# A four-stage transformer kernel: weighting moved ahead of a placing in the delta-rule stage, and the last layer's first transpositions moved ahead of a projection

## The chip, the cores and the metric

The kernel runs on one core of one Trainium2 chip. The time is the device time of one execution in microseconds (us). It was run three times for the median, and one further execution was profiled. The profile names the engines of the core: PE (TensorE, matrix products), DVE (VectorE), ACT (ScalarE), POOL (GpSimd), and SP, which only issues transfers. Each engine runs its own instructions strictly in the order of its queue, and the engines meet through semaphores, so a wait at the head of a queue holds everything behind it.

## The reference, cut to what matters

Four layers run one after the other over 2048 tokens of 128 features (two batches of 1024 tokens): an attention, a gated feed-forward network, a delta-rule layer with convolutions, and a network of sign weights. Each is followed by a residual addition and a layer norm. The change touches the third layer and the first steps of the fourth.

```python
# third layer; per batch and head: L = 1024 tokens in 32 chunks of 32 tokens
def body(S, inp):                       # a scan over the 32 chunks
    q_i, k_i, u_i, w_i = inp
    attn = jnp.where(tri, jnp.einsum('bhcd,bhed->bhce', q_i, k_i), 0.0)
    u_i = u_i - w_i @ S
    o_i = q_i @ S + attn @ u_i
    S = S + jnp.einsum('bhcd,bhce->bhde', k_i, u_i)
    return (S, o_i)
...
local_short = causal_dwconv(vf, fir_short)      # filter of 3 taps over the values
local_long = causal_dwconv(vf, fir_long)        # filter of 31 taps
p = jax.nn.softmax(logits, axis=-1)
local_mix = p[..., 0:1] * v + p[..., 1:2] * local_short + p[..., 2:3] * local_long
o = w_global[..., None] * delta_out + (1.0 - w_global)[..., None] * local_mix
o = o * jax.lax.rsqrt(jnp.mean(o * o, -1, keepdims=True) + EPS) * rms_w
x = _layernorm(x + o.reshape(Bx, Lx, H * DV) @ Wo)
# fourth layer
h = jnp.concatenate([x, -x], axis=-1)
h = s0 * _conn_dense(k0, h)             # weights +1 or -1 from k0; then relu, two more products
```

## The kernel before, in words

All instructions are written out by hand, one list for each engine, with explicit semaphores; no scheduler changes their order. The two batches of the delta rule go through the same steps, first batch 0, then batch 1. For one batch, in the order of the data:

1. PE multiplies by the inverse matrices (`times_inverse`, L1893), ACT copies the result, called u and w, to SBUF (`copy_uw`, L746).
2. DVE and ACT place the u parts into a block layout, one half each (`place_u`, L524), and PE forms the inputs of the state (`inputs_of_state`, L1903), which ACT copies out (`copy_b`, L753).
3. PE forms the products of the transitions (L1914). DVE makes the matrix of each step and corrects the queries from them (`transitions`, L1331 and L1336).
4. PE starts the outputs of batch 0 (`begin_outputs`, L1927, four groups of 16 products ahead of the scan).

Then one scan of 31 steps serves both batches: in each step PE multiplies the state (L1994), DVE adds the step's input (L1445; step 0 is the copy L1442), and PE puts products of outputs behind each state product (L1961 and L1927). The scan can begin when DVE has made its first copy, L1442.

Beside this path lies the local mix. The filters' results stand in `filtered` in token layout. DVE multiplies their weights in (`weigh(i)`, L1345, two instructions of 128x512 for each of four groups of 512 tokens; the groups come in the order `FINAL = (0, 2, 1, 3)`, so `weigh(0)` and `weigh(1)` serve the token groups 0 and 2). POOL multiplies the values by their weights (L1019, four instructions), and adds the two filters to them (L1029 and L1030, two instructions for each group). What comes of this is first used late in the scan, by `blend_local`. DVE also forms the first sign weights of the last layer, `sw0` (L1356).

Toward the end of the scan and behind it, for each group i of tokens: ACT and DVE norm the outputs, PE transposes them (`o_to_features`, L1974), ACT copies them (`load_oT`, L798), PE projects (`project`, L1983, two instructions for each of four tiles), DVE adds the residual and takes the statistics (`add_y4` L1390, `stats3` L1396 and L1399), POOL forms the reciprocal root, and DVE norms (`norm3`, L1407). The last layer then begins with PE's transpositions (`x3_transposes`, L2034), which ACT and DVE split into a leading part and a rest (`transposed`, L802 on ACT, L1418 on DVE). PE's first products are `first` (L2044, L2045) and `hidden` (L2056, L2057), with ACT's relu (L807) and DVE's rest (`rests`, L1423) between them. For group 0 the transposed rows use the bank in which `o_to_features` writes, so PE waits there for `oT_ready` 2 as well as for `x3_ready` 1.

## Time and profile before

| | |
|---|---|
| median of three runs | 609.99 us |
| lowest and highest | 609.53 and 613.34 us |
| the profiled execution's own time | 612.65 us |
| its span, first to last instruction | 610.9 us |
| busy in the span: PE, DVE, ACT, POOL | 545.2, 406.9, 324.7, 175.1 us |
| the chain that ended last, by engine | PE 71%, DVE 10%, DMA 7%, ACT 7%, issue 3% |
| mean granted clock of PE | 0.932 of full |

The profiled execution lies 2.66 us above the median, and 1.75 us of its time lie outside its span. Busy times are means over stages with different limits, so they don't tell what a change in one stage is worth. In the rows below, a row of the timeline gives the start, the duration, the engine, the line of the kernel, what is written and read, the number of instructions that are merged in it, and in square brackets the idle time ahead of it with what ended it.

### The profile page before, as it was taken

What the parts mean: (1) busy time and instruction counts of PE and PEld (TensorE: products, weight loads), DVE (VectorE), ACT (ScalarE), POOL (GpSimd) and SP (SyncE); (2) the same over time, 40 slices, a digit from 0 to 9 for tenths busy, and PEclk for the clock granted to TensorE, in tenths of its full rate; (3) what the DMA queues carried; (4) which work ended last, traced back from release to release, by engine and by line L of the source; (5) the groups of instructions that cost most, each with busy time, mean ns of one, the idle gap of its engine ahead of it and who ended that gap; (6) DMA issues with size and microseconds to landing.
All of it is one profiled execution on the core that took longest, in us unless ns stands there. A gap on an engine that the chain in (4) does not pass through costs nothing.

```text
span 610.9 us, 17361 instructions
## 1 busy us (share of the span) xinstructions
PE 545.2 (89%) x7412; PEld 377.7 (62%) x7412; DVE 406.9 (67%) x773; ACT 324.7 (53%) x574; POOL 175.1 (29%) x333
## 2 busy tenths in 40 slices
PE   4699999999999999999999996996998659888993
PEld 2345555555555557877777774774676658666672
DVE  5697989999999825263634437447798572576774
ACT  2327888887888875656555544656605300134441
POOL 7000111445445421010101024238980370010101
PEclk9999999999999999999999998997999665559998
DMA  4778657374250000010000000032734100000011
GB/s 116 149 216 208 191 142 162 68 162 67 62 100 4 5 2 1 0 28 10 0 2 1 1 0 1 2 70 38 139 75 85 23 3 4 5 1 0 2 34 34
DMA packets 54050, 33.80 MB, mean 55 GB/s; under 512 B 38853, under 2 KB 45509, under 8 KB 53974
## 3 DMA queue, kind: packets, MB, share of 16 engines
q1 hardware_dynamic: 48822, 31.65, 23.0%
q10 hardware_dynamic: 5152, 1.05, 1.1%
q8 instruction: 58, 0.95, 0.7%
q14 instruction: 18, 0.15, 0.1%
HBM read 20.83 MB, written 9.44 MB: 50 GB/s over the span
## 4 chain that ended last, share of the span: by engine, by line
PE 71%; DVE 10%; DMA 7%; ACT 7%; issue 3%; SPq 1%; POOL 1%; POOLq 0%; ACTq 0%; DVEq 0%
PE ps L1761 9%; PE ps L1746 8%; PE ps L1513 7%; PE ps L1515 6%; PE ps L1514 6%; PE ps L1861 6%; DMA qst<-shift_sb 5%; PE ps L1725 3%; PE ps L1927 2%; PE ps L2056 2%; PE ps L2057 2%; PE ps L1893 2%; ACT prob L682 2%; PE ps L1994 2%; PE ps L1603 1%
## 5 line engine op out<-in xcount | busy, mean ns | idle before, releaser
L1204 DVE TENSOR_REDUCE nmx<-ps 128x1 f32<-128x1024 f32 x128 | 154.1, 1217 | 19.4 <-PE ps L1726 17.9
L682 ACT ACTIVATE prob<-ps 128x512 f32<-128x512 f32 x256 | 137.5, 597 | 27.0 <-PE ps L1746 26.8
L1761 PE MATMUL ps<-prob,vp 128*32 128x128 f32 x2048 | 78.9, 278 | 0.0
L1746 PE MATMUL ps<-qst,kst 50*128 50x512 f32 x256 | 73.6, 492 | 4.9 <-ACT prob L682 3.4
L1761 PEld LDWEIGHTS ps<-prob,vp 128*32 128x32 f32 x2048 | 49.1, 109 | 39.8 <-ACT prob L682 22.6
L1077 DVE TENSOR_TENSOR h_lo<-hf,h_hi 128x512 fp32r<-128x512 f32 x48 | 33.1, 689 | 52.5 <-ACT h_hi L591 50.2
L1513 PE MATMUL ps<-h_hi,w_lo 128*128 128x512 f32 x144 | 58.2, 404 | 2.4 <-DVE h_lo L1077 2.4
L1515 PE MATMUL ps<-h_hi,w_hi 128*128 128x512 f32 x144 | 56.9, 395 | 0.0
L1514 PE MATMUL ps<-h_lo,w_hi 128*128 128x512 f32 x144 | 56.8, 394 | 0.0
L1725 PE MATMUL ps<-kst,qst 48*128 48x512 f32 x128 | 53.0, 415 | 3.4 <-DMA kst<-k_scratch 3.3
L1726 PE MATMUL ps<-kst,qst 48*128 48x512 f32 x128 | 51.7, 405 | 0.0
L1746 PEld LDWEIGHTS ps<-qst,kst 50*128 50x128 f32 x256 | 29.3, 183 | 35.0 <-ACT prob L682 22.9
L590 ACT ACTIVATE hf<-ps,ffn_scale 128x512 f32<-128x512 f32 x32 | 22.1, 690 | 34.3 <-PE ps L1515 32.7
L852 POOL TENSOR_SCALAR rs<-mv 128x4 f32<-128x4 f32 x8 | 3.0, 376 | 122.4 <-DVE mv L1055 122.3
L1861 PE MATMUL ps<-vpad,fir_diag 32*32 32x512 f32 x1088 | 37.0, 618 | 0.4 <-DVE ka L1139 0.4
L891 POOL CAST nsplit<-nmx 128x4 fp32r<-128x4 f32 x32 | 6.0, 188 | 106.7 <-DVE nmx L1204 104.4
L1513 PEld LDWEIGHTS ps<-h_hi,w_lo 128*128 128x128 f32 x144 | 27.0, 188 | 11.6 <-issue 4.0
L1423 DVE SCALAR_TENSOR_TENSOR h_lo<-ps,h_hi 128x512 fp32r<-128x512 f32 x32 | 21.2, 684 | 16.4 <-ACT h_hi L807 16.4
L1861 PEld LDWEIGHTS ps<-vpad,fir_diag 32*32 32x32 f32 x1088 | 23.9, 105 | 12.3 <-issue 3.8
L1515 PEld LDWEIGHTS ps<-h_hi,w_hi 128*128 128x128 f32 x144 | 27.0, 188 | 6.7
L1514 PEld LDWEIGHTS ps<-h_lo,w_hi 128*128 128x128 f32 x144 | 27.1, 188 | 6.0
L807 ACT ACTIVATE h_hi<-ps 128x512 fp32r<-128x512 f32 x32 | 18.0, 598 | 23.2 <-PE ps L2057 18.0
(248 smaller groups left out, 1107.5 us busy)
## 6 DMA issues: line engine op xcount, KB each, us to landing
qst<-q_scratch SPq DMA_DIRECT2D x31, 192.0 KB, 4.4
kst<-k_scratch SPq DMA_DIRECT2D x31, 192.0 KB, 5.0
w_raw<-L_ffn_h_w SPq DMA_DIRECT2D x8, 256.0 KB, 3.4
kd<-ka SPq DMA_DIRECT2D x8, 256.0 KB, 6.2
X<-L_attn_x SPq DMA_DIRECT2D x4, 256.0 KB, 5.3
qst<-shift_sb SPq DMA_DIRECT2D x64, 4.0 KB
q_scratch<-w_hi SPq DMA_DIRECT2D x2, 512.0 KB, 5.5
k_scratch<-w_lo SPq DMA_DIRECT2D x2, 512.0 KB, 3.1
```

The source lines that it names most:

```text
L590: nc.scalar.activation(hf[:, o, :], bank, ACT.Gelu, scale=scale)
L682: nc.scalar.activation(prob[:, n % PROBS, GT * (t % 2):GT * (t % 2) + GT], ps[:, RINGB + i % RING, :], ACT.Exp, scale=SCORE_SCALE).then_in ...
L1077: nc.vector.tensor_tensor(h2_lo[:, layer, o, :], hf[:, o, :], h2_hi[:, layer, o, :].bitcast(F32), ALU.subtract).then_inc(lo2_ready, 1)
L1204: nc.vector.tensor_reduce(nmx[:, u % 2, j:j + 1], pair, AX.X, ALU.max, negate=True).then_inc(max_done, 1)
L1513: nc.tensor.matmul(out, wl, xh, start=start, stop=False)
L1514: nc.tensor.matmul(out, wh, xl, start=False, stop=False)
L1515: return nc.tensor.matmul(out, wh, xh, start=False, stop=stop)
L1725: nc.tensor.matmul(ps[:, bank, :], qst[0:48, p, P * k:P * k + P], kst[0:48, p, 0:GT], start=True, stop=True)
L1726: nc.tensor.matmul(ps[:, bank + 1, :], qst[64:112, p, P * k:P * k + P], kst[64:112, p, GT:S], start=True, stop=True).then_inc(max_psum, 1)
L1746: nc.tensor.matmul(ps[:, RINGB + i % RING, :], kst[r:r + 50, p, P * t:P * t + P], half_of(qst[r:r + 50, p, :], u % 2), start=True, stop=Tr ...
L1761: last = nc.tensor.matmul(ps[32 * j:32 * j + 32, PVB, P * half:P * half + P], vp[:, h, t, :], prob[:, n % PROBS, c:c + P], start=(t == 0), ...
L1861: last = nc.tensor.matmul(ps[32 * g:32 * g + 32, FIR_BANK[k] + h, :], fir_diag[f, (0, FIRL)[k] + t, :], vpad[f, g // 2, off:off + GT], sta ...
```

## The change

Nothing is computed differently; instructions change places in three of the queues.

```diff
@@ POOL: the memset of the state and the wait for the corrected queries
-            pool.wait_ge(uw_psum, B)
-            nc.gpsimd.memset(state[:, 0], 0.0).then_inc(state_zeroed, 1)
-            pool.wait_ge(g_ready, 2)
             for i, g in enumerate(FINAL):
+                if i == 2:
+                    pool.wait_ge(uw_psum, B)
+                    nc.gpsimd.memset(state[:, 0], 0.0).then_inc(state_zeroed, 1)
+                    pool.wait_ge(g_ready, 2)
@@ DVE: before the scan
             weigh(0)
             weigh(1)
+            weigh(2)
+            weigh(3)
+            dve.wait_ge(signs_in, 16 * 6)
+            nc.vector.tensor_tensor(sw0[:], k0[:, 0, :], k0[:, 1, :], ALU.subtract)
             place_u(nc.vector.tensor_copy, dve, 1, (2, 3))
             transitions(1)
-            dve.wait_ge(signs_in, 16 * 6)
-            nc.vector.tensor_tensor(sw0[:], k0[:, 0, :], k0[:, 1, :], ALU.subtract)
-            weigh(2)
-            weigh(3)
@@ DVE: behind the scan
             norm3(0)
+            transposed(0)
             add_y4(1)
             stats3(1)
-            transposed(0)
             rests(0, 0, range(FB))
@@ PE: in the scan
-                if j == 29:
+                if j == 28:
                     project(0, (0, 1))
-                if j == 30:
+                if j == 29:
                     project(0, (2, 3))
@@ PE: behind the scan
+            x3_transposes(0)
             project(1, (0, 1, 2, 3))
-            x3_transposes(0)
             first(0)
```

On DVE, ahead of the scan, the queue of the kernel before reads as follows. `low<-inv_flat` is `place_u` of batch 1, `sw` is the last layer's sign weights, and `state<-prep` is the scan's first step.

```order
L1345 TENSOR_TENSOR filtered<-filtered,mixw 128x4x4x32 x3
L524 COPY low<-inv_flat 32x32x32 [waits b_psum0,low_zeroed0,uw_ready0]
L524 COPY low<-inv_flat 32x32x32
L1331 TENSOR_TENSOR tT<-eye,ps 128x256 [waits mg_psum0]
L1331 TENSOR_TENSOR tT<-eye,ps 128x256 x3
L1336 TENSOR_TENSOR kq<-kq,ps 128x8x32 x4
L1356 TENSOR_TENSOR sw<-k 128x512 [waits x_in1]
L1345 TENSOR_TENSOR filtered<-filtered,mixw 128x4x4x32 x4
L1442 COPY state<-prep 128x64 [waits b_ready0]
```

The same place in the changed kernel (line numbers are one higher there):

```order
L1346 TENSOR_TENSOR filtered<-filtered,mixw 128x4x4x32 x7
L1357 TENSOR_TENSOR sw<-k 128x512 [waits x_in1]
L524 COPY low<-inv_flat 32x32x32 [waits b_psum0,low_zeroed0,uw_ready0]
L524 COPY low<-inv_flat 32x32x32
L1332 TENSOR_TENSOR tT<-eye,ps 128x256 [waits mg_psum0]
L1332 TENSOR_TENSOR tT<-eye,ps 128x256 x3
L1337 TENSOR_TENSOR kq<-kq,ps 128x8x32 x4
L1443 COPY state<-prep 128x64 [waits b_ready0]
```

Four weighting instructions and the one on the signs have moved from between the transitions and the first state to ahead of the placing.

On POOL, in the same stretch, the kernel before has the memset ahead of all additions of the filters:

```order
L1019 TENSOR_TENSOR vtok<-vtok,mixw 128x512 x3
L1024 MEMSET state 128x64 [waits uw_psum0,pool_step]
L1029 TENSOR_TENSOR vtok<-vtok,filtered 128x512 [waits weighted0,g_ready0]
L1030 TENSOR_TENSOR vtok<-vtok,filtered 128x512 [waits pool_step]
L1029 TENSOR_TENSOR vtok<-vtok,filtered 128x512 [waits weighted0]
```

The changed kernel there:

```order
L1019 TENSOR_TENSOR vtok<-vtok,mixw 128x512 x3
L1030 TENSOR_TENSOR vtok<-vtok,filtered 128x512 [waits weighted0,pool_step]
L1031 TENSOR_TENSOR vtok<-vtok,filtered 128x512 [waits pool_step]
L1030 TENSOR_TENSOR vtok<-vtok,filtered 128x512 [waits weighted0]
L1031 TENSOR_TENSOR vtok<-vtok,filtered 128x512 [waits pool_step]
L1026 MEMSET state 128x64 [waits uw_psum0]
L1030 TENSOR_TENSOR vtok<-vtok,filtered 128x512 [waits weighted0,g_ready0]
```

Four of the eight additions now stand ahead of the memset and need only `weighted`.

On PE, behind the scan, the kernel before projects group 1 (`ps<-wo,vk`) and then transposes the normed rows (`ps<-ident,X`):

```order
L1974 MATMUL ps<-ident,low 128x128 x3
L1983 MATMUL ps<-wo,vk 128x128 [waits y4_added0,oT_ready0]
L1983 MATMUL ps<-wo,vk 128x128 x3
L2034 MATMUL ps<-ident,X 128x128 [waits oT_ready0,x3_ready0]
L2034 MATMUL ps<-ident,X 128x128 x3
L2044 MATMUL ps<-x_lo,sw 128x512 [waits x3T_lo0,x3T_hi0]
```

The changed kernel there:

```order
L1975 MATMUL ps<-ident,low 128x128 x3
L2035 MATMUL ps<-ident,X 128x128 [waits oT_ready0,x3_ready0]
L2035 MATMUL ps<-ident,X 128x128 x3
L1984 MATMUL ps<-wo,vk 128x128 [waits y4_added0,oT_ready0]
L1984 MATMUL ps<-wo,vk 128x128 x3
L2045 MATMUL ps<-x_lo,sw 128x512 [waits x3T_lo0,x3T_hi0]
```

The wait for the normed rows now stands ahead of the projection of group 1.

## Rows read from the trace of the kernel before

**Rows 1.** Timeline of DVE ahead of the scan, 424 to 530 us.

```profile
473.93 5.10 DVE L1345 TENSOR_TENSOR filtered<-filtered,mixw 128x512 f32<-128x512 f32 x4
486.21 1.39 DVE L524 COPY low<-inv_flat 32x1024 f32<-32x1024 f32 x2 [7.19 <-ACT inv_flat L746]
...
488.96 1.40 DVE L1336 TENSOR_TENSOR kq<-kq,ps 128x256 f32<-128x256 f32 x4
490.29 0.68 DVE L1356 TENSOR_TENSOR sw<-k 128x512 fp32r<-128x512 uint8 x1
490.89 6.76 DVE L1345 TENSOR_TENSOR filtered<-filtered,mixw 128x512 f32<-128x512 f32 x4
497.57 1.25 DVE L1442 COPY state<-prep 128x64 f32<-128x64 f32 x1
```

**Rows 2.** Timeline of PE in the same stretch.

```profile
490.51 0.54 PE L1927 MATMUL ps<-inv_flat,kd 64*64 64x32 f32 x12 [0.66 <-DVE kq L1336]
491.81 1.70 PE L1927 MATMUL ps<-inv_flat,kd 64*64 64x32 f32 x52 [0.76 <-issue]
498.96 0.44 PE L1994 MATMUL ps<-state,tT 32*32 32x32 f32 x16 [5.45 <-DVE state L1442]
```

**Rows 3.** Timeline of ACT, ahead of the scan and at its end.

```profile
489.89 1.20 ACT L753 COPY prep<-ps 128x256 f32<-128x256 f32 x4 [1.58 <-PE ps L1903]
...
530.18 0.59 ACT L798 COPY vk<-ps 128x512 f32<-128x512 f32 x1 [1.74 <-PE ps L1974]
```

**Rows 4.** Timeline of POOL ahead of the scan and at its start.

```profile
474.15 5.80 POOL L1019 TENSOR_TENSOR vtok<-vtok,mixw 128x512 f32<-128x512 f32 x4 [16.66 <-DVE kq L1336]
...
490.44 1.65 POOL L1029 TENSOR_TENSOR vtok<-vtok,filtered 128x512 f32<-128x512 f32 x1 [6.08 <-DVE kq L1336]
...
501.42 1.27 POOL L1030 TENSOR_TENSOR vtok<-vtok,filtered 128x512 f32<-128x512 f32 x1
```

**Rows 5.** Windows: busy us of five engines, then granted PE clock, DMA share, GB/s.

```profile
484.00:493.00 9.00, 5.35 (x311) 4.74 (x311) 6.75 (x13) 5.34 (x10) 2.63 (x3) 1.00 0.02 5
493.00:494.00 1.00, 0.51 (x17) 0.40 (x13) 1.00 (x1) 0.00 (x0) 1.00 (x2) 0.72 0.00 0
499.00:542.00 43.00, 37.13 (x1212) 30.98 (x1212) 18.30 (x67) 4.17 (x9) 5.37 (x7) 0.50 0.02 4
542.00:548.00 6.00, 5.86 (x14) 4.63 (x15) 3.52 (x8) 2.39 (x4) 0.81 (x1) 0.50 0.01 3
548.00:560.00 12.00, 9.77 (x50) 7.50 (x48) 7.41 (x14) 6.77 (x15) 0.00 (x0) 1.00 0.00 0
```

**Rows 6.** The chain that ended last, in a step of the scan: start, us, what.

```profile
505.54 0.57 PE ps L1927 x8
```

**Rows 7.** Timeline of PE at the end of the scan and behind it.

```profile
531.29 1.22 PE L1983 MATMUL ps<-wo,vk 128*128 128x128 f32 x4
...
532.87 1.22 PE L1983 MATMUL ps<-wo,vk 128*128 128x128 f32 x4
...
537.23 2.08 PE L1983 MATMUL ps<-wo,vk 128*128 128x128 f32 x8 [0.67 <-ACT vk L798]
539.10 1.06 PE L2034 MATMUL ps<-ident,X 128*128 128x128 f32 x4
542.14 0.76 PE L2044 MATMUL ps<-x_lo,sw 128*128 128x512 f32 x1 [1.98 <-DVE x_lo L1418]
```

**Rows 8.** Timeline of DVE in the same stretch.

```profile
532.95 0.23 DVE L1445 TENSOR_TENSOR state<-ps,prep 128x64 f32<-128x64 f32 x1 [1.35 <-PE ps L1994]
...
537.63 1.12 DVE L1407 TENSOR_SCALAR X<-X,mv,rs 128x128 f32<-128x128 f32 x4 [0.20 <-POOL rs L1036]
539.35 0.69 DVE L1390 TENSOR_TENSOR X<-X,ps 128x512 f32<-128x512 f32 x1 [0.60 <-PE ps L1983]
...
541.27 0.72 DVE L1418 SCALAR_TENSOR_TENSOR x_lo<-ps,s_sign,x_lo 128x512 fp32r<-128x512 f32 x1
544.00 0.69 DVE L1423 SCALAR_TENSOR_TENSOR h_lo<-ps,h_hi 128x512 fp32r<-128x512 f32 x1 [2.00 <-ACT h_hi L807]
```

More of the change, by code:

```diff
@@ L2016, in _ @@
                     o_to_features(0, (2, 3))
+                if j == 28:
+                    project(0, (0, 1))
                 if j == 29:
-                    project(0, (0, 1))
-                if j == 30:
                     project(0, (2, 3))
```

## The prediction, made before the changed kernel ran

> **What bounds the kernel now.** I first read the chain of waits, to find who holds the stage that the change touches. Ahead of the scan it passes from PE to DVE: through `transitions(1)`, the sign weights, the second weighting, and the first copy of the state, and only then back to PE. The timelines of the engines show the same. DVE ends L1336 at 490.36, then works for 0.68 us on the signs, 6.76 us on the weighting and 1.25 us on the copy [rows 1]. PE has ended its last product ahead of the scan at 493.51, and waits 5.45 us for that copy [rows 2]. The inputs of the state have been with DVE since 491.09 [rows 3]. So the 7.4 us on signs and weighting are on the path only as far as they reach past PE's own work, 5.45 us. The reader should also see the hole on DVE before that: from 479.03 to 486.21 it waits 7.19 us for ACT's copies [rows 1]. That is where the change puts this work.
>
> The second thing to see is that DVE and POOL hold each other up. A 128x512 instruction with two operands in SBUF took 0.68 us when it began ahead of POOL's addition (the signs, L1356); the weighting, of the same size, took 6.76/4 = 1.69 us each beside POOL's additions and 5.10/4 = 1.28 us beside POOL's L1019 [rows 1, 4]. POOL's addition takes 1.65 us beside DVE's weighting and 1.27 us when DVE leaves it alone [rows 4].
>
> The third view is the clock of PE. It is granted at 1.00 (2.4 GHz) from 484 to 493, falls within the microsecond from 493 to 494 (mean 0.72), and stays at 0.50 (1.2 GHz) through the whole scan and behind it until 548, from where it is 1.00 again [rows 5]. A mean of 0.72 puts the fall at 493 + (0.72 - 0.5)/0.5 = 493.4, ahead of the 5.45 us of idleness. So it is not this idleness that brings it down.
>
> **Part 1, the weighting and the signs ahead of the placing.** On DVE they begin at 479.03. POOL's last L1019 is then still running, until 479.95 [rows 4]. Then POOL starts its four additions of groups 0 and 1, whose weights are in; in the kernel before they waited for `g_ready` 2 until 490.44. This is the part of the move that the gap doesn't show: five instructions of DVE that would need 5 x 0.68 = 3.4 us alone stand beside five of POOL's. At the measured pace of a pair, 1.65 to 1.69 us, POOL's four end at 479.95 + 4 x 1.67 = 486.6. The signs, as DVE's fifth, are held by the fourth addition and end most of their own 0.68 us behind it, an estimate of 487.1. The placing began at 486.21, so it is 0.9 us later. Its bounds: nothing, if DVE isn't held up beyond 486.2 (five at the 1.28 us of the L1019 rows end at 485.4), and 1.3 us if all five take 1.69 us (487.5). I take 0.9, because L1029 and L1030 are the very instructions that POOL runs there.
>
> Beside the measured pace stands a rule of the Trainium skill. Its page "SBUF — State Buffer", section "SBUF: two separate sides", says that the port pair which DVE and POOL share is locked for a whole instruction, and that the loser fully blocks. By that rule a pair takes the sum of both engines' own times, 0.68 + 1.27 = 1.95 us, which is rival A below. The trace agrees with the direction and not quite with the size: 1.65 to 1.69 us for a pair.
>
> The placing on DVE moves to 487.1 to 488.5. ACT's half of it ended at 488.31 anyway, so PE's L1903 is 0.2 us later and the inputs of the state are ready near 491.3. The transitions follow the placing: from its start to the end of L1336 it was 490.36 - 486.21 = 4.15 us, now 487.1 + 4.15 = 491.25. PE's 64 products of L1927 therefore begin at 491.4 instead of 490.51, and need 3.0 us with the 0.76 us gap that they have [rows 2]: to 494.4. The state's copy is only 64 columns wide. It took 1.25 us since POOL was in the midst of an addition; in the worst case it takes the same now, from 491.3 to 492.6, and hides behind L1927. POOL's memset comes behind its four additions, near 486.8, and PE asks for it only behind L1927. The scan starts at about 494.45 instead of 498.96: **-4.5 us**.
>
> One thing takes part of it back. If the clock falls at 493.4 as before, what is left of L1927 (1.0 us) runs at half rate: 8 of them take 0.57 us, 71 ns each [rows 6], against 1.70/52 = 33 ns each. That is +1.1 us. It cost nothing in the kernel before, because 5.45 us of waiting covered it. When the fall comes nearly a whole L1927 earlier, the price is 64 x 38 ns = 2.4 us; when it comes later, 0. I take half of 1.1 us, **+0.6**.
>
> The scan itself keeps its instructions and, by the rows, its clock of 0.50. POOL's last four additions, now 1.27 us each with nothing beside them, end early in the scan, long before `blend_local` needs them. The state additions of DVE took 0.23 us with or without POOL.
>
> **Part 2, project(0) one step earlier.** The step-28 place on PE is reached at 530.7. ACT's copy of what is projected ends at 530.77 [rows 3], so PE waits about 0.15 us there. Moreover the last addition of the state was hidden under the second projection: DVE did it from 532.95 to 533.18 while PE projected until 534.02 [rows 7, 8]. With both projections gone from there, PE waits 0.2 us for it. In return, the projection is out before the last addition, so `add_y4(0)` starts right behind it: 534.3 instead of 534.12. The sum is 0.2 us later for the residual path and 0.3 for PE: **+0.2**.
>
> **Part 3, transpositions ahead of project(1), and transposed(0) ahead of add_y4(1).** Before, PE projected group 1 from 537.23, while DVE normed group 0 (537.63 to 538.75), transposed until 540.16, and then waited 1.98 us for L1418, which stood behind `add_y4(1)` and its statistics on DVE, 539.35 to 541.35 [rows 7, 8]. Now PE waits from about 536.9 for the norm, to 538.95, transposes in 1.06 us, projects in 2.08 us, and is at 542.05. ACT and DVE have split the rows by 541.6 meanwhile. `first(0)` thus begins at 542.05 against 542.14. The 1.98 us wait is gone, and a wait of about the same length ahead of the transpositions has taken its place; PE has the same work between the norm and the first product. Behind that, `add_y4(1)` and the statistics (2.0 us) now run from 542.1 to 544.1; the first `rests` was ready at 544.00 [rows 8], so 0.1 us at most comes back. This part is **-0.1** (part 2's 0.2 us are already in those times, so both together are -0.1). Its bounds: +0.4, if `rests` is late for all of `hidden`, and -1.5, if the clock returns sooner because PE now works from 539 on without a pause.
>
> **The sum.** -4.5 + 0.6 - 0.1 = -4.0 us. Against the profiled execution's own 612.65 us this gives 608.6; it lies 2.66 us above the median, and nothing in the terms depends on that offset, so against the median it is 609.99 - 4.0 = **606.0 us**, 0.7% faster.
>
> **Rivals.**
>
> A. *The contention eats more* (0.15). Each of DVE's five instructions waits for a whole addition of POOL: five pairs of 0.68 + 1.27 = 1.95 us from 479.03 end at 488.8, and the placing is late by 2.6 us instead of 0.9. For it: POOL's additions now stand exactly in DVE's old hole. Against: the pairs of before took 1.69 us. The gain is 4.0 - 1.7 = 2.3 us, **607.7 us**.
>
> B. *The clock stays at 2.4 GHz into the scan* (0.10). The only long idleness of PE ahead of the scan goes. Products of L1927 would then take 33 ns instead of 71 in the first steps and the 16 with eight each, (48 + 128) x 38 ns = 6.7 us less at the most, of which I take 4 to be on the path, since part of it would only turn into waiting for DVE's addition. That gives **602 us**. Against: the clock fell before that idleness, and 43 us of scan in which PE was busy for 37.13 us did not bring it back [rows 5]. The Trainium skill, "TensorE: Matmul & The Clock Gate", section "What's actually happening", holds that activity releases the throttle and that the gate follows how busy PE has been. By that rule removing the idleness should keep the clock; the trace of the scan doesn't agree with its simple form, as small products that fill PE's row leave the clock at 0.50.
>
> C. *Nothing is gained* (0.08): the changed order does what it says, but the scan's early steps turn out to wait for something else, as for the inputs of the state, or the time comes back in the dense products behind the scan, which DVE's and ACT's chain bounds. **610 us**.
>
> D. *Slower* (0.05). The clock's return moves back. From 542 to 548 PE did 14 wide products in 5.86 us, 0.42 each, which at the full rate would be 0.21; and the clock returned only after these unbroken products from 542.14 on [rows 5, 7]. If the new wait ahead of the transpositions, with `rests` behind `add_y4(1)`, breaks that row up, each product at the lower rate costs 0.21 us. More than 19 of them cancel the 4 us; 33 would give -4 + 7 = +3, **613 us**. Against: the new order makes PE's row from the transpositions on longer, not shorter.
>
> **How the numbers follow.** The forecast has 0.62; within it the unknown terms (0 to 1.3 for the port, 0 to 2.4 for the clock, -1.5 to +0.4 for part 3) spread it from 603.5 to 608. For 8 in 10 I add rival A and most of B above 602: **602.0 to 609.0**. A measurement of this kernel can tell about 1% (6 us) from no change. Faster by more than that, below 603.9, is B and an eighth of the forecast case, with some of the noise: 0.20. Slower by that is D: 0.04. The rest, 0.76, is within 1%.
>
> **What would show it right or wrong.** In the changed profile: no wait of PE for L1443 above 1 us; DVE without its 7.19 us hole, its weighting at about 1.7 us each, and POOL's additions from 480 to 486.6; the placing near 487; the scan's first L1995 at 494 to 496; the clock at 0.50 through the scan; a wait of about 2 us ahead of L2035, and none ahead of L2045. I would be wrong above all if the clock in the scan is not 0.50, or if the port makes the placing later than 488.

## The result

The changed kernel took 606.17 us in the median of seven runs (604.1 to 607.3), against 609.99 us before, also in seven runs. The ratio is 0.9915, with a 95% interval from 0.9892 to 0.9938. That is 0.85% or 5 us less by the ratio and 3.8 us by the medians: a real gain, and one within the 1% that the prediction named. Ratios here and below leave disturbed runs out, so they can differ a little from the quotient of two medians.

The profiled execution of the changed kernel took 606.14 us with a span of 604.4, so 6.5 us less than the profiled one of before. The first thing to do with such a pair is to cut it at a place ahead of the change. ACT's second copy of u and w begins at 481.82 here; it began at 484.12 before (DVE's placing, right behind it, at 486.21 [rows 1]). That 2.30 us arose in parts that the change doesn't touch, and it is nearly the offset of the profiled execution of before above its median. From here on all stages are counted from this copy. Its row before:

```profile
484.12 2.05 ACT L746 COPY inv_flat<-ps 128x512 f32<-128x512 f32 x4 [7.99 <-PE ps L1893]
```

DVE ahead of the scan, in the changed kernel (timeline; all line numbers are one higher than before):

```profile
471.87 11.61 DVE L1346 TENSOR_TENSOR filtered<-filtered,mixw 128x512 f32<-128x512 f32 x8
483.40 1.77 DVE L1357 TENSOR_TENSOR sw<-k 128x512 fp32r<-128x512 uint8 x1
485.18 1.39 DVE L524 COPY low<-inv_flat 32x1024 f32<-32x1024 f32 x2
```

The hole of 7.19 us of before [rows 1] is gone: eight weightings in one row, the signs, and at once the placing. The signs took 1.77 us where they had taken 0.68. ACT's copies were out at 481.82 + 2.05 = 483.87; the placing begins at 485.18, so it is 1.3 us late.

POOL and ACT in the same stretch (two timelines):

```profile
472.10 5.79 POOL L1019 TENSOR_TENSOR vtok<-vtok,mixw 128x512 f32<-128x512 f32 x4 [16.79 <-DVE kq L1337]
477.97 1.60 POOL L1030 TENSOR_TENSOR vtok<-vtok,filtered 128x512 f32<-128x512 f32 x1
...
483.00 1.61 POOL L1031 TENSOR_TENSOR vtok<-vtok,filtered 128x512 f32<-128x512 f32 x1
...
489.42 1.27 POOL L1030 TENSOR_TENSOR vtok<-vtok,filtered 128x512 f32<-128x512 f32 x1 [4.72 <-DVE kq L1337]
```

```profile
481.82 2.05 ACT L746 COPY inv_flat<-ps 128x512 f32<-128x512 f32 x4 [8.39 <-PE ps L1894]
```

The first four additions lie from 477.97 to 484.61, at 1.6 to 1.7 us; the later ones, with nothing of DVE beside them, take 1.27 us, as in [rows 4].

PE ahead of the scan and the windows of its clock (busy us of five engines, granted clock, DMA share, GB/s):

```profile
486.62 1.69 PE L1904 MATMUL ps<-low,ka 64*32 64x64 f32 x128 [2.02 <-DVE low L524]
489.49 3.63 PE L1928 MATMUL ps<-inv_flat,kd 64*64 64x32 f32 x64 [1.18 <-DVE kq L1337]
493.04 0.44 PE L1995 MATMUL ps<-state,tT 32*32 32x32 f32 x16
```

```profile
484.00:493.00 9.00, 5.80 (x234) 5.30 (x224) 6.44 (x12) 3.20 (x6) 4.21 (x5) 0.70 0.01 4
...
499.00:536.00 37.00, 31.62 (x1065) 25.85 (x1064) 15.64 (x55) 4.17 (x9) 1.29 (x2) 0.50 0.02 4
```

PE no longer waits ahead of L1995; the 5.45 us of [rows 2] are gone. Its 64 products now run wholly at the lower clock, since the clock had fallen by then (a mean of 0.70 over the nine us from 484 puts the fall at 487.6): 3.55 us from their first to the scan, against 3.0 us with a gap inside before. From ACT's copy to the scan it is 11.22 us, against 14.84 before: 3.62 us less. The scan runs at 0.50 as before [rows 5].

The end of the scan and behind it, PE and then DVE:

```profile
533.03 1.11 PE L2035 MATMUL ps<-ident,X 128*128 128x128 f32 x4 [1.99 <-DVE X L1408]
533.94 1.92 PE L1984 MATMUL ps<-wo,vk 128*128 128x128 f32 x8
535.80 0.76 PE L2045 MATMUL ps<-x_lo,sw 128*128 128x512 f32 x1
```

```profile
523.71 0.22 DVE L1446 TENSOR_TENSOR state<-ps,prep 128x64 f32<-128x64 f32 x1 [1.40 <-PE ps L1995]
...
528.22 0.23 DVE L1446 TENSOR_TENSOR state<-ps,prep 128x64 f32<-128x64 f32 x1 [1.35 <-PE ps L1995]
528.37 0.68 DVE L1391 TENSOR_TENSOR X<-X,ps 128x512 f32<-128x512 f32 x1
...
531.86 1.12 DVE L1408 TENSOR_SCALAR X<-X,mv,rs 128x128 f32<-128x128 f32 x4 [0.20 <-POOL rs L1037]
534.91 0.75 DVE L1419 SCALAR_TENSOR_TENSOR x_lo<-ps,s_sign,x_lo 128x512 fp32r<-128x512 f32 x1 [1.93 <-ACT x_lo L802]
```

The residual's addition now follows the last state addition at once (528.37 behind 528.22); before it came 1.17 us behind it (534.12 against 532.95 [rows 8]). But the last steps are longer: the addition of step 27 (523.71) and the last one are 4.51 us apart, against 3.41 before (from 529.54 to 532.95). PE's wait of 1.99 us stands ahead of the transpositions, and the first wide product begins at 535.80 without a wait, 3.94 us behind the start of the norm. Before it was 542.14 - 537.63 = 4.51 us [rows 7, 8].

So the 6.5 us between the two profiles are: 2.30 ahead of the change, 3.62 up to the scan, 0.42 from the scan to the first wide product (43.18 us before, 42.76 now), and 0.16 from there to the end.

One thing behind the first wide product did change. The granted clock came back to 1.00 3.0 us behind that product, where it had taken 5.9 us before [rows 5]:

```profile
538.00:539.00 1.00, 1.00 (x4) 0.78 (x3) 0.96 (x2) 0.74 (x2) 0.92 (x2) 0.59 0.00 0
```

It fell once more, at 549.1, and was back at 552.5; before, it stayed at 1.00 there. From the first wide product to the end of the span it is 68.6 us now and 68.8 before.

### The profile page after: what moved, and what is told of

It is laid out like the page before. It is cut to its first block, busy times and chain, and to the rows that moved or that the text cites. A ratio compares the mean times of both kernels' runs of the same rounds, so it can differ in the third digit from the quotient of the medians.

```text
span 604.4 us, 17361 instructions
## 1 busy us (share of the span) xinstructions
PE 547.1 (91%) x7412; PEld 381.0 (63%) x7412; DVE 406.5 (67%) x773; ACT 325.0 (54%) x574; POOL 174.7 (29%) x333
## 4 chain that ended last, share of the span: by engine, by line
PE 72%; DVE 12%; ACT 6%; DMA 5%; issue 2%; POOL 1%; SPq 1%; POOLq 0%; ACTq 0%; DVEq 0%
PE ps L1762 10%; PE ps L1747 9%; PE ps L1514 7%; PE ps L1516 6%; PE ps L1515 6%; PE ps L1862 6%; DMA qst<-shift_sb 3%; PE ps L1928 3%; PE ps L1726 3%; PE ps L2057 2%; PE ps L2058 2%; DVE filtered L1346 2%; ACT prob L682 2%; PE ps L1995 1%; PE ps L1604 1%
```

## The experiments

Ten kernels. For each profile the same two stretches are read: from the start of ACT's second copy of u and w to the scan (**A**), and from there to the first wide product of the last layer (**B**). Two more columns give the clock of PE, from windows of 0.5 us: when it fell, counted from the same copy, and when it was back at 1.00, counted from the first wide product (below zero: ahead of it). The results of all are in one table, the readings behind it.

| kernel | ratio to before | 95% interval | A, us | placing behind ACT's copy started, us | B, us | clock fell, us | clock back, us |
|---|---|---|---|---|---|---|---|
| before | 1 | | 14.84 | 2.09 | 43.18 | 9.3 | 5.9 |
| changed | 0.9915 | 0.9892 to 0.9938 | 11.22 | 3.36 | 42.76 | 5.8 | 3.0 |
| e1, part 1 alone | 0.9931 | 0.9906 to 0.9957 | 9.43 | 2.09 | 42.78 | 9.1 | 4.7 |
| e2, parts 2 and 3 alone | 0.9979 | 0.9948 to 1.001 | 14.84 | 2.08 | 42.39 | 11.2 | 1.8 |
| e3, POOL as before | 0.9926 | 0.99 to 0.9952 | 10.73 | 2.09 | 42.10 | 9.4 | 0.9 |
| e4, filling ahead of the scan | 0.9912 | 0.988 to 0.9945 | 10.61 | 3.28 | 41.51 | 9.3 | 1.5 |
| e5, 512 columns a step | 1.0242 | 1.0216 to 1.0269 | 11.80 | 3.94 | 60.63 | 5.7 | 1.6 |
| e6, 256 columns a step | 1.0144 | 1.0116 to 1.0172 | 10.49 | 3.12 | 55.29 | 8.8 | 1.1 |
| e7, projection first | 0.9949 | 0.9929 to 0.9969 | 11.60 | 3.74 | 43.38 | 5.7 | -1.5 |
| e8, part 2 alone | one execution, 613.05 us | | 14.85 | 2.09 | 42.70 | 6.1 | 3.2 |
| e9, POOL's part alone | 0.9962 | 0.9937 to 0.9987 | 11.65 | 2.09 | 42.64 | 9.1 | 6.0 |
| e10, signs behind | 0.9919 | 0.9889 to 0.9948 | 9.63 | 2.09 | 42.08 | 8.9 | 1.5 |

Read A with care. The changed kernel, e1, e5, e6 and e7 have the same instructions up to the scan, and their A is 11.22, 9.43, 11.80, 10.49 and 11.60 us. A difference of up to some 2 us between two single profiles therefore shows nothing by itself. The three kernels with the old order up to the scan (before, e2, e8) all have 14.84 or 14.85 us.

**e1_part1: the work ahead of the scan alone.** The diffs on POOL and on DVE ahead of the scan, and nothing of the rest.

> Only the work ahead of the scan is moved: the second weighting and the signs ahead of the placing on DVE, four of POOL's additions ahead of its memset; all of the order behind the scan is that of the kernel before. Theory 1 (the gain comes from DVE's hole, and parts 2 and 3 are worth a few tenths): about 3.6 us faster than before, 606.4, the scan begins at about 494, and the first product of the last layer waits near 2 us for DVE's rest, as before. Theory 2 (a good part of the gain comes from the order behind the scan, because PE's clock returns sooner there): no more than 2.5 us faster, 607.5 or above.

0.9931, or 4.2 us less than before: the greater part of the change's gain. In the profile the first wide product waits 1.97 us for DVE's rest, as before. Theory 2, at most 2.5 us (a ratio of 0.9959), falls just outside the interval, which ends at 0.9957. A is 9.43 us, 1.8 less than in the changed kernel. DVE and PE of e1:

```profile
486.56 1.76 DVE L1357 TENSOR_TENSOR sw<-k 128x512 fp32r<-128x512 uint8 x1
488.58 1.39 DVE L524 COPY low<-inv_flat 32x1024 f32<-32x1024 f32 x2 [0.27 <-ACT inv_flat L746]
```

```profile
492.88 0.54 PE L1928 MATMUL ps<-inv_flat,kd 64*64 64x32 f32 x12 [0.66 <-DVE kq L1337]
494.17 1.82 PE L1928 MATMUL ps<-inv_flat,kd 64*64 64x32 f32 x52 [0.75 <-issue]
```

The weighting and signs took just as long (11.61 and 1.76 us). But here ACT's copy began 11.5 us behind the first weighting, against 9.95 us in the changed kernel, since PE had started its products with the inverse later. The hole was long enough, the placing waited for ACT and not for DVE, and PE's 64 products fell under the higher clock for the most part. The same code therefore loses between nothing and 1.9 us (e5's placing: 3.94 - 2.09) to the shared access, according to when the copies come.

**e2_parts23: the rest of the change alone.**

> The complement: the order ahead of the scan is that of the kernel before, the projections of group 0 stand one step earlier, and the transpositions of the last layer stand ahead of the projection of group 1. Theory 1: 0 to 0.4 us faster than before, 609.6 to 610. Theory 2: 1.3 us faster or more, 608.7 or below, with the granted clock back at 1.00 about 3 us sooner behind the first product than before.

0.9979, an interval that includes 1. The ratios alone can't settle it. The profile can: from the norm to the first wide product it takes 3.94 us (538.69 to 542.63), exactly as in the changed kernel and 0.57 less than before, and from the addition of step 27 to the norm 8.15 us against 8.09. So parts 2 and 3 are worth 0.5 us there, more than theory 1 had allowed and less than theory 2. The sign that theory 2 named did show: the clock was back 1.8 us behind the first wide product, 4.1 us sooner than before. But it fell again 12 us behind that product, which it did not do before, and from the first wide product to the end of the span e2 took 68.9 us, against 68.8.

**e3_pool_late: POOL in its old order.** In the changed kernel:

```diff
+            pool.wait_ge(uw_psum, B)
+            nc.gpsimd.memset(state[:, 0], 0.0).then_inc(state_zeroed, 1)
+            pool.wait_ge(g_ready, 2)
             for i, g in enumerate(FINAL):
-                if i == 2:
-                    pool.wait_ge(uw_psum, B)
-                    nc.gpsimd.memset(state[:, 0], 0.0).then_inc(state_zeroed, 1)
-                    pool.wait_ge(g_ready, 2)
```

> The changed kernel, but POOL keeps its old order: memset, the wait for the second correction of the queries, and then all eight additions. DVE's weighting then has only POOL's last multiplication beside it in the hole. Theory 1 (the shared access of DVE and POOL delays the placing by about 1.2 us in the changed kernel): the four weightings and the signs take 0.7 to 1.3 us each instead of 1.6 to 1.8, the placing begins as soon as ACT's copies are out, and the kernel is 0.5 to 1.2 us faster than the changed one, 605.0 to 605.7. Rival: the delay is hidden behind PE's products or paid back where POOL's eight additions meet the state's first copy: the same as the changed kernel, 606.2.

DVE of e3 (timeline):

```profile
473.94 8.38 DVE L1345 TENSOR_TENSOR filtered<-filtered,mixw 128x512 f32<-128x512 f32 x8
482.24 0.68 DVE L1356 TENSOR_TENSOR sw<-k 128x512 fp32r<-128x512 uint8 x1
487.90 1.39 DVE L524 COPY low<-inv_flat 32x1024 f32<-32x1024 f32 x2 [4.98 <-ACT inv_flat L746]
```

Without POOL's additions the eight weightings take 8.38 instead of 11.61 us and the signs 0.68 instead of 1.77; 4.98 us of the hole are left. This shows that the additions are what holds DVE up: 4.3 us over five instructions. The placing isn't late. Yet A is 10.73 us, where e1, whose placing wasn't late either, has 9.43. PE's 64 products have a gap of 1.58 us inside, for which the profile names no releaser (0.76 us in [rows 2], 0.75 in e1), and the last 52 of them took 2.29 us instead of 1.82, since more of them lay behind the fall of the clock. Those two make the 1.3 us. The ratio, 0.9926, does not tell e3 from the changed kernel; the 0.5 to 1.2 us that theory 1 expected are not shown.

**e4_fill_ahead: PE kept busy ahead of the scan.**

```diff
+            def keep_busy(n):
+                for _ in range(n):
+                    nc.tensor.matmul(ps[:, 0, 256:512], sw1[:, 0, 0:P], sw1[:, 1, 0:256], start=True, stop=True)
...
             transition_products(1)
+            keep_busy(16)
             inputs_of_state(1)
```

> The changed kernel with 16 more products of 128x256 on PE, whose results nobody reads, in the wait for the placed u blocks ahead of the inputs of the state. They fill some 1.7 us of idleness of PE at the full clock. If the fall of the clock ahead of the scan follows PE's idle time just before it: the 64 products that begin the outputs run at 1.00 and take 2.2 to 3.0 us instead of 3.6, and the kernel is up to 1.4 us faster than the changed one, 604.8 to 606. If small products keep the clock down whatever stands before them: the same or up to 0.3 us slower, 606.2 to 606.5, with the scan at 0.50 in either case.

```profile
485.32 2.18 PE L1934 MATMUL ps<-wc_parts 128*128 128x256 f32 x16
487.43 1.45 PE L1904 MATMUL ps<-low,ka 64*32 64x64 f32 x125
490.43 0.30 PE L1904 MATMUL ps<-low,ka 64*32 64x64 f32 x3 [1.56 <-issue]
490.66 2.62 PE L1928 MATMUL ps<-inv_flat,kd 64*64 64x32 f32 x64
```

```profile
482.00:491.00 9.00, 6.67 (x302) 5.91 (x298) 7.99 (x13) 4.38 (x7) 4.21 (x4) 1.00 0.01 4
491.00:493.00 2.00, 2.00 (x60) 2.00 (x56) 0.79 (x1) 0.97 (x4) 1.92 (x3) 0.73 0.04 8
```

The clock stayed at 1.00 until PE was in the midst of L1928, which took 2.62 us instead of 3.63. That agrees with a fall that answers to what PE did just before, but doesn't show that the filling did it. In the changed kernel, e5 and e7, PE had waited 2.0 to 2.6 us ahead of L1904, and the clock fell 5.7 to 5.8 us behind the start of ACT's copy. In e6, with the same instructions up to the scan and no filling, it had waited 1.78 us, and the clock fell at 8.8 us, nearly as late as here (9.3). And before, e2 and e8 have the same order up to the scan and the same wait of 1.46 us, and the clock fell at 9.3, 11.2 and 6.1 us. A shortens by 0.6 us only, for a gap of 1.56 us, again with no releaser, fell into L1904. From 493 to 536 the mean clock is 0.50 all the same. The ratio, 0.9912, is that of the changed kernel within the noise.

**e5_scan_fill512 and e6_scan_fill256: a wide product in every step.** In the changed kernel, behind the state product of each step (256 instead of 512 in e6):

```diff
                 last.then_inc(state_psum, 1)
+                if j < 26:
+                    nc.tensor.matmul(ps[:, 3, 0:512], sw1[:, 0, 0:P], sw1[:, 1, 0:512], start=True, stop=True)
```

> The changed kernel with one more product of 128x512 in each step of the scan before the 26th (25 in all), behind the state product, into a bank that nobody reads then. Their results are not used. The question is what holds PE's clock at 0.50 in the scan. Theory 1 (it is the narrow products of 32 columns, which leave it down however closely they follow each other): with a wide product in every step the clock comes back to 1.00 within the first steps and stays; the added products cost 25 x 0.21 us = 5.3 us at the full clock, while the steps with L1928 lose up to 0.2 to 0.3 us each, the stretch behind the scan up to the first dense products some 3 us: between 3 us faster and 1 us slower than the changed kernel, 603 to 607. Rival (the scan's clock doesn't answer to a wide product a step): each costs 0.43 us, up to 10 us slower, 612 to 617, with 0.50 throughout.

> As the run with 512 columns, but 256 columns in each of the 25 added products; half the cost, and half the activity. Theory 1: if half is enough, the clock comes back as well, and the time is 2.6 us below that of the run with 512 columns; if it isn't, 0.50 throughout and 25 x 0.21 = 5 us above the changed kernel, 611. Rival: 0.50 throughout in both runs, and this one about 5 us above the changed kernel.

The windows of e5, and then of e6:

```profile
500.00:540.00 40.00, 40.00 (x843) 26.91 (x847) 7.90 (x29) 1.16 (x3) 0.00 (x0) 0.50 0.01 3
```

```profile
493.00:530.00 37.00, 37.00 (x822) 28.90 (x821) 5.17 (x22) 0.00 (x0) 2.01 (x2) 0.50 0.01 3
```

The clock stays at 0.50 in both, with PE busy without a pause. Theory 1 of these two runs falls, and with it the hope of a scan at 2.4 GHz by such means. The rivals were right on the clock and too low on the price: they gave 612 to 617 us and about 611 us, and the ratios come to 624.8 and 618.8 us. One step of e5 on PE, and one of the changed kernel behind it:

```profile
506.96 0.64 PE L1928 MATMUL ps<-inv_flat,kd 64*64 64x32 f32 x8
507.52 0.43 PE L1995 MATMUL ps<-state,tT 32*32 32x32 f32 x16
507.89 0.80 PE L1998 MATMUL ps<-wc_parts 128*128 128x512 f32 x1
508.61 0.44 PE L1962 MATMUL ps<-state,kq 32*32 32x32 f32 x16
508.98 0.64 PE L1928 MATMUL ps<-inv_flat,kd 64*64 64x32 f32 x8
```

```profile
499.54 0.64 PE L1928 MATMUL ps<-inv_flat,kd 64*64 64x32 f32 x8
500.11 0.28 PE L1995 MATMUL ps<-state,tT 32*32 32x32 f32 x4
500.16 0.27 PE L1962 MATMUL ps<-state,kq 32*32 32x32 f32 x3
...
500.53 0.64 PE L1928 MATMUL ps<-inv_flat,kd 64*64 64x32 f32 x8
```

A step takes 2.03 us instead of 0.99, counted between DVE's additions, so the product of 512 columns costs 1.04 us, where 14 wide products in a row take 0.42 us each at this clock [rows 5]. The rows show where the rest goes. In the changed kernel the 16 products of the state (L1995) and the 16 of the outputs (L1962) run interleaved and need 0.42 us together, from 500.11 to 500.53. In e5 the wide product stands between them, and each group needs 0.37 us by itself: 0.32 us more. The wide product holds the row for 0.72 us, from 507.89 to 508.61, and not for 0.42: 0.30 us more. With 256 columns a step takes 1.81 us, 0.82 more. Over the whole of B the 25 products cost 17.9 us (0.71 each) and 12.5 us (0.50 each), since not every step is lengthened as much.

**e7_project_first: PE's old order, DVE's new one.** In the changed kernel:

```diff
-            x3_transposes(0)
             project(1, (0, 1, 2, 3))
+            x3_transposes(0)
```

> The changed kernel, but PE projects group 1 first and transposes behind it, as in the kernel before; DVE keeps the new order, its rest of the transposed rows ahead of the addition and the statistics. Theory 1 (PE's wait of 2 us ahead of the transpositions is what the new order on PE brings, and its wait ahead of the first product came from DVE's order alone): the projection fills that wait, and the first product begins 0.2 to 0.4 us sooner behind the norm of group 0 than in the changed kernel, 3.5 to 3.7 us instead of 3.94; in the whole time no difference that can be measured, 605.8. Rival (the new order on PE was needed): 4.2 us or more from the norm to the first product.

PE of e7, then DVE:

```profile
533.28 2.08 PE L1984 MATMUL ps<-wo,vk 128*128 128x128 f32 x8 [0.67 <-ACT vk L798]
535.16 1.06 PE L2035 MATMUL ps<-ident,X 128*128 128x128 f32 x4
537.87 0.47 PE L2045 MATMUL ps<-x_lo,sw 128*128 128x512 f32 x1 [1.66 <-DVE x_lo L1419]
```

```profile
533.43 1.12 DVE L1408 TENSOR_SCALAR X<-X,mv,rs 128x128 f32<-128x128 f32 x4 [0.20 <-POOL rs L1037]
...
536.98 0.75 DVE L1419 SCALAR_TENSOR_TENSOR x_lo<-ps,s_sign,x_lo 128x512 fp32r<-128x512 f32 x1 [2.42 <-ACT x_lo L802]
```

From the norm to the first wide product: 537.87 - 533.43 = 4.44 us. My expectation of 3.5 to 3.7 failed, the rival's held. The projection does fill PE's wait, but it keeps PE until 535.2, when the norm has been done for 0.6 us, and behind the transpositions nothing is left to hide the split on ACT and DVE, 1.66 us of waiting. In the changed kernel the projection lies over that split. So the new order on PE is what gives the 0.57 us; DVE's new order alone gives 0.07. The whole time is 0.9949 of before, against 0.9915 for the changed kernel: the intervals overlap, so the 2 us between them are not shown, and no more than about 1 us of them lies in A and B (0.38 and 0.62).

**e8_part2: the projections one step earlier, alone.**

> The kernel before with the two projections of group 0 one step earlier and nothing else. Theory 1: from the state addition of step 27 to the norm of group 0 it takes as long as before, 8.1 us, give or take 0.2, since what the later steps lose the start of the residual's addition gains; the whole time is within its spread of the kernel before. Rival: part 2 alone is worth 0.5 us or more there.

From the addition of step 27 (529.72) to the norm (537.86) it takes 8.14 us, against 8.09 before. Part 2 is worth nothing, as theory 1 had it.

**e9_pool_only: POOL's new order with DVE's old one.**

> The kernel before with POOL's new order alone: the additions of groups 0 and 1 ahead of the memset. DVE keeps its order, signs and second weighting behind the transitions. Theory 1 (the work that DVE moved is what counts): the four weightings are still on the path; but POOL now waits for the third group's weights, so the first two of them run beside nothing at 0.68 us and the last two at about 1.7 us, and the way from ACT's second copy of u and w to the scan falls from 14.8 us to 12 to 12.8 us; 2 to 2.8 us faster than before, ratio 0.995 to 0.9965. Rival (POOL's order is only there so that DVE's could change): 14.8 us and no gain. Rival 2 (POOL's order brings nearly all of the gain): 11.2 us or less, and a ratio near 0.9915.

POOL, DVE and PE of e9:

```profile
476.98 1.26 POOL L1030 TENSOR_TENSOR vtok<-vtok,filtered 128x512 f32<-128x512 f32 x1
...
489.19 1.58 POOL L1030 TENSOR_TENSOR vtok<-vtok,filtered 128x512 f32<-128x512 f32 x1 [6.94 <-DVE filtered L1346]
```

```profile
487.76 3.56 DVE L1346 TENSOR_TENSOR filtered<-filtered,mixw 128x512 f32<-128x512 f32 x4
```

```profile
492.64 0.44 PE L1995 MATMUL ps<-state,tT 32*32 32x32 f32 x16 [1.63 <-DVE state L1443]
```

A is 11.65 us, 3.19 less than before, with DVE's work still behind the transitions. The four weightings take 3.56 us instead of 6.76 [rows 1], because POOL has nothing to add until the third group is weighted. The whole time is 0.9962 of before. All of the 3.2 us can't be added to what DVE's move gives: PE waits 1.63 us for DVE here, and no more than that was left to gain from moving the weighting and the signs. A is shorter than theory 1 had reckoned (12 to 12.8) and longer than rival 2 asked (11.2 or less). The whole time, 0.9962, lies in the range of theory 1 and not near the 0.9915 of rival 2.

**e10_signs_behind: the signs kept behind the transitions.** In the changed kernel:

```diff
-            dve.wait_ge(signs_in, 16 * 6)
-            nc.vector.tensor_tensor(sw0[:], k0[:, 0, :], k0[:, 1, :], ALU.subtract)
             place_u(nc.vector.tensor_copy, dve, 1, (2, 3))
             transitions(1)
+            dve.wait_ge(signs_in, 16 * 6)
+            nc.vector.tensor_tensor(sw0[:], k0[:, 0, :], k0[:, 1, :], ALU.subtract)
```

> The changed kernel, but the instruction on the signs stays behind the transitions on DVE, where it lies beside PE's 64 products that begin the outputs. Theory 1 (it is DVE's fifth instruction beside POOL's additions that makes the placing late, and PE's products cover 0.7 us behind the transitions): the placing begins at most 0.2 us behind ACT's copies, and the scan 9.4 to 10.7 us behind the start of those copies, against 11.2 in the changed kernel; in the whole time 0 to 0.8 us faster than the changed kernel, which is within what a measurement can tell. Rival (the copy of the state, now behind the signs, becomes the last thing that the scan waits for): 11.2 us or more.

```profile
486.60 2.03 DVE L524 COPY low<-inv_flat 32x1024 f32<-32x1024 f32 x2 [0.46 <-ACT inv_flat L746]
...
491.31 0.68 DVE L1359 TENSOR_TENSOR sw<-k 128x512 fp32r<-128x512 uint8 x1
491.92 1.25 DVE L1443 COPY state<-prep 128x64 f32<-128x64 f32 x1
```

The placing begins with ACT's last copy, though ACT's copies came just as soon behind the weighting as in the changed kernel (9.97 us behind the first weighting). It lasts 2.03 us, for POOL's last addition still overlaps it. The state's copy ends at 493.17, a microsecond ahead of the scan at 494.14, so it isn't the last. A is 9.63 us, 1.6 less than in the changed kernel. Of that, 0.95 us is the clock, which in e10 fell late enough for L1928 to take 2.68 us instead of 3.63; only the other 0.64 us comes from the order of the signs: the placing began 1.27 us sooner and took 0.64 us longer. In the whole time, 0.9919 against 0.9915, nothing shows: 1.6 us is about half the width of either interval.

## Why the prediction was right, point by point

**The time.** 606.0 us was forecast and 606.17 measured, within the range and within 1% as given the greatest chance. Part of this closeness is luck, as the points show.

**Part 1, where the gain is.** Right: PE waited 5.45 us for DVE, the wait is gone, and A is 3.62 us shorter where -4.5 + 0.6 = -3.9 was forecast. e1 shows that this part carries the gain. That the two numbers come so close is in part luck, since A of the same instructions lies between 9.43 and 11.80 us.

**The port.** Right in mechanism and near in size: the placing was to be 0.9 us late and was 1.27 us late (3.36 - 2.09). POOL's additions ended at 484.61, 6.7 us behind L1019, as worked out. e3 shows the cause by taking the additions away. What the prediction missed is that the term isn't a constant: it was 0 in e1, 1.03 to 1.85 in e6 and e5, with the same instructions. It depends on how soon ACT's copies follow the weighting. In the changed kernel, e4, e5, e6 and e7 DVE begins the placing 13.3 us behind its first weighting every time, while ACT's copy begins anywhere from 9.36 to 10.20 us behind it; in e1 it began 11.47 us behind it, and nothing was lost. The rule of the Trainium skill that a held instruction waits for the whole of the other ("SBUF — State Buffer", "SBUF: two separate sides") was rival A with 2.6 us. Pairs took 1.6 to 1.7 us here too, not 1.95, so its direction is confirmed and its strict sum is not.

**What in part 1 brings it.** Incomplete. I treated POOL's move as a burden on DVE's move only. It is a gain of its own: alone it shortens A by 3.2 us, since it takes POOL's additions off the time in which DVE weights on the path. DVE's move alone, with POOL late (e3), shortens A by 4.1 us. Either one does most of it; together they can't give more than the 5.45 us that PE waited.

**The clock.** Right in direction: the fall came ahead of the scan although the 5.45 us of idleness were gone, the scan stayed at 0.50, and the lower clock reached into PE's 64 products. The price was 0.55 us against 0.6 forecast, but by another way: all 64 ran at 0.50, at 55 ns each (3.55/64) and not at the 71 ns that I took from the scan's groups of eight, and the 0.76 us gap inside them was absent. At 33 ns each they would have taken 2.1 us, so the clock cost 1.4 us and the absent gap gave more than half of it back; that the net came to the forecast is luck. Nor was the fall where the prediction left it: it came at 5.8 us behind the start of ACT's copy and not at 9.3, and other executions of the same instructions had it at 5.7 (e5, e7), 8.8 (e6) and 9.1 us (e1). Rival B, a scan at 2.4 GHz, falls: neither the missing idleness nor a wide product a step brought the clock back. The Trainium skill's sentence that activity releases the throttle ("TensorE: Matmul & The Clock Gate", "What's actually happening") is not borne out in its simple form by e5, where PE was busy for 40 of 40 us at 0.50. e4, where the fall came late behind the filling, agrees with it but doesn't show it, since in e6 the fall came nearly as late without filling. What in those steps fails to count as activity, no run here separates.

**Part 2.** The direction was right, the step longer and the residual's addition sooner, and nothing left over: 8.15 us against 8.09 from step 27 to the norm, where +0.2 was forecast. e8 alone gives 8.14.

**Part 3.** A wait of about 2 us ahead of L2035 in place of the one ahead of the first wide product: right, 1.99 for 1.98. The size was too small: 0.57 us gained from norm to product, where the times given imply 0.3 (from 538.95 - 1.12 to 542.05 is 4.22, against 4.51). Parts 2 and 3 together gave -0.5 for -0.1 (43.18 to 42.76 in B, 0.42; 0.57 behind the norm, less what was lost up to it). The transpositions and the projection behind each other took 2.77 us from the first to the wide product, not the 3.1 of their separate rows.

**The clock's return.** The prediction gave it a bound of -1.5 us in part 3 and, moving back, rival D. D falls: the clock was back 3.0 us behind the first wide product instead of 5.9. In every kernel with the new order behind the scan it came sooner (0.9 to 3.0 us; -1.5 in e7, where DVE's order is new there and PE's isn't) than in those with the old one (3.2 to 6.0: before, e1, e8, e9). The gain of it was small at most: from the first wide product to the end of the span it is 68.2 to 68.9 us in all twelve profiles, and in seven of them, the changed kernel among them, the clock fell again for a while, 11.8 to 13.4 us behind that product.

**The offset.** The prediction assumed that the 2.66 us by which the profiled execution lay above its median had nothing to do with the change. The cut at ACT's copy bears that out: 2.30 us of the difference of the two profiles lie ahead of it.

## What to carry to other kernels

Work that a waiting engine could do in a hole is worth no more than the wait behind it: look up what the last waiter would wait for next, here PE's own products. When two engines share an access, moving either one's work out of the critical stretch helps by itself; try the engine that has the slack first, and leave out of the hole whatever other work already covers, as the signs here (e10 has the placing on time; in the whole time it can't be told apart). And cut two profiles at a point ahead of the change before comparing them: a third of the difference here lay there.

## What the hardware showed unexpectedly

A 128x512 product put between the 32x32 products of a step lengthened the step by 1.04 us (256 columns: 0.82 us), while 14 such products in a row take 0.42 us each at the same clock. Doubling the columns cost 0.22 us, about half of the 0.42 us of a whole wide product; the other 0.6 us come at both widths. Half of them (0.32 us) is that the two groups of 16 narrow products no longer run interleaved. The other half (0.30 us) is time that the wide product takes beyond its own 0.42, with narrow products ahead of and behind it; the runs don't say why.

PE's stream of small products has gaps for which the profile names no releaser. In the 64 products ahead of the scan the gap was 0.76, 0.75, 1.06, 1.58, 0.16, 0.28, 1.02 us (before, e1, e2, e3, e6, e8, e9) and absent in the changed kernel, e4, e5, e7 and e10. It alone can move A by over a microsecond, as much as the variants that were to be told apart. Its place is always the same: behind the 12th of the 64 products. In e4, where 16 more products stand ahead, the gap is behind the 125th of the 128 products of L1904, 15 products sooner in the order. So it goes with a place in PE's sequence of instructions and not with one of the products; what PE waits for there, no run here shows.

The clock of PE fell at very different times in executions of the same instructions: 6.1, 9.3 and 11.2 us behind the start of ACT's copy in e8, before and e2, which are the same up to the scan.
